# Regrouping the result operands of a two-layer adapter kernel: rank rows of both layers per half, expert rows apart, layer-0 rows gathered by GpSimd

## What is computed

```python
def layer(x, A, B, ids, W, b, eA, eB, rW):           # cut
    c = einsum('bnr,bor->bno', einsum('bni,bri->bnr', x, B[ids]), A[ids])   # rank 16
    alpha = softmax(einsum('bth,eh->bte', c, rW) + const)                   # 4 experts
    z = einsum('bth,erh->bter', c, eA)                                      # rank 8
    return x + c @ W.T + b + 2 * einsum('bter,eor,bte->bto', z, eB, alpha)
x = layer(x, layer 0: 8 adapters, ids 3..7)
x = layer(x, layer 1: 64 adapters, ids 4..50)
```

## Time and profile before

| | |
|---|---|
| time, 3 runs | 365.12 us median, 362.91 to 365.51 |
| profiled execution | span 359.3 us from the first to the last instruction |
| PE busy | 313.8 us, 87% of the span, mean granted clock 0.962 |
| DVE, ACT, POOL busy | 68%, 42%, 25% |
| DMA | 56.15 MB, mean 156 GB/s |

### The profile page before, as it was taken

How to read it: one execution, slowest core, us unless ns; L and a number is a source line. 1 busy time by engine, 2 the same in 40 slices (tenths; PEclk the granted TensorE clock), 3 DMA queues, 4 the chain that set the end, 5 groups by cost and what they waited for, 6 DMA issues and landing times.

```text
span 359.3 us, 6465 instructions
## 1 busy us (share of the span) xinstructions
PE 313.8 (87%) x2056; PEld 296.2 (82%) x2056; DVE 242.6 (68%) x496; ACT 149.4 (42%) x317; POOL 89.6 (25%) x61
## 2 busy tenths in 40 slices
PE   0936568889997999799979999999989998999975
PEld 0935568789997999699979998999989998999854
DVE  5914975788566864787397848784768566864564
ACT  5856833762065404650166206620573065402310
POOL 0014520193015500460026202530244015500000
PEclk9978858969999999999999999999999999999999
DMA  7899426712781078305950387029801880041005
GB/s 284 311 281 332 149 88 200 230 41 68 238 301 40 14 238 288 108 1 156 288 200 0 116 278 249 0 75 298 260 11 51 270 285 36 0 175 61 0 0 234
DMA packets 31524, 56.15 MB, mean 156 GB/s; under 512 B 3793, under 2 KB 21074, under 8 KB 31506
## 3 DMA queue, kind: packets, MB, share of 16 engines
q1 hardware_dynamic: 31506, 55.94, 46.7%
HBM read 39.15 MB, written 16.78 MB: 156 GB/s over the span
## 4 chain that ended last, share of the span: by engine, by line
issue 45%; PE 16%; POOL 14%; DVE 9%; SPq 6%; ACT 4%; DMA 4%; POOLq 0%; ACTq 0%; DVEq 0%
POOL xs_lo L909 12%; PE ps_d L318 4%; PE ps_d L320 3%; PE ps_d L319 3%; POOL a1s_lo L909 2%; DMA abraw<-ab_tab 2%; SPq L222 1%; DMA xraw<-x_in 1%; DVE w1s_lo L676 1%; SPq L233 1%; DVE xs_lo L676 1%; PE ps_h L325 1%; DVE bst_lo L676 1%; SPq L235 1%; ACT m1x_hi L512 1%
## 5 line engine op out<-in xcount | busy, mean ns | idle before, releaser
L909 POOL TENSOR_TENSOR xs_lo<-xraw,xs_hi 128x512 fp32r<-128x512 f32 x48 | 67.7, 1424 | 205.9 <-ACT xs_hi L512 205.9
L318 PE MATMUL ps_d<-w1s_hi,a1s_hi 128*128 128x384 f32 (+1 forms) x216 | 73.4, 340 | 9.5 <-DVE w1s_lo L676 9.5
L320 PE MATMUL ps_d<-w1s_hi,a1s_lo 128*128 128x384 f32 (+1 forms) x216 | 71.3, 330 | 0.0
L319 PE MATMUL ps_d<-w1s_lo,a1s_hi 128*128 128x384 f32 (+1 forms) x216 | 71.0, 329 | 0.0
L895 DVE SCALAR_TENSOR_TENSOR xraw<-ps_d,bsum,xraw 128x512 f32<-128x512 f32 x62 | 46.2, 750 | 26.1 <-PE ps_d L320 26.1
L318 PEld LDWEIGHTS ps_d<-w1s_hi,a1s_hi 128*128 128x128 f32 x216 | 42.3, 196 | 10.1 <-issue 8.4
L318 PE MATMUL ps_p<-xs_hi,bst_hi 128*128 128x256 f32 x128 | 39.4, 307 | 7.4 <-DVE xs_lo L676 3.6
L512 ACT ACTIVATE xs_hi<-xraw 128x512 fp32r<-128x512 f32 x64 | 37.3, 622 | 14.1 <-PE ps_p L320 8.5
L319 PEld LDWEIGHTS ps_d<-w1s_lo,a1s_hi 128*128 128x128 f32 x216 | 42.0, 195 | 0.0
L320 PEld LDWEIGHTS ps_d<-w1s_hi,a1s_lo 128*128 128x128 f32 x216 | 41.8, 194 | 0.0
L319 PE MATMUL ps_p<-xs_lo,bst_hi 128*128 128x256 f32 x128 | 37.9, 296 | 0.0
(11 more groups left out here) (154 smaller groups left out, 661.5 us busy)
## 6 DMA issues: line engine op xcount, KB each, us to landing
xraw<-x_in SPq DMA_DIRECT2D x32, 512.0 KB, 5.9
out<-xraw SPq DMA_DIRECT2D x32, 512.0 KB, 3.8
xraw<-w SPq DMA_DIRECT2D x16, 512.0 KB, 6.1
abraw<-ab_tab SPq DMA_DIRECT2D x64, 128.0 KB, 2.5
b0raw<-b_tab SPq DMA_DIRECT2D x64, 64.0 KB, 2.3
b0raw<-a SPq DMA_DIRECT2D x1, 512.0 KB, 3.6
lp<-exp SPq DMA_DIRECT2D x4, 69.0 KB, 7.3
cm<-exp_in SPq DMA_DIRECT2D x1, 144.0 KB, 6.6
```

Source lines behind the costliest of these rows:

```text
L318: pe.matmul(acc, lh, rh, start=first, stop=False, skip_group_check=True)
L319: pe.matmul(acc, lh, rl, start=False, stop=False, skip_group_check=True)
L320: return pe.matmul(acc, ll, rh, start=False, stop=final, skip_group_check=True)
L909: return pool.tensor_tensor(dst, whole, high.bitcast(F32), ALU.subtract)
```

## The change

- The row operands are regrouped. `res` holds, for each half, 128 rank rows: 64 of layer 1 (made in the step, as before) and 64 of layer 0, of the adapters that the 4 sequences of the half use. Their coefficients are `cf` (c1 in the rows of layer 1, c0 in those of layer 0), two buffers that alternate by step. The scattered `k1` is still made, for `route(0)` and `q`.
- The expert rows stand apart: `ew_hi` has the 64 expert rows twice, `ew_lo` their low parts and 64 zero rows; `ce` holds the high parts of the 64 coefficients and below them the low parts. So the expert part of a tile is two 512-column matmuls, and that of `q` too (`hle`).
- A result tile is thus 2 x 3 matmuls of 256 columns and 2 of 512 (before: 3 of 512 and 6 of 256); `q` is 3 + 2 of 512 (before 3 of 512 and 6 of 256).
- The layer-0 rows go once to a table in DRAM (`m0_tab`, 1 MB), and GpSimd gathers them: in each step, once PE has ended the results of the step before (`d_done`), it loads 8 adapter numbers to registers and issues 8 DMAs of 16 rows x 8 KB (128 KB), ahead of its low parts of x.
- The `start_results` tiles now need c1, so in the last step all five stand behind `route(1)`. ACT and DVE write an expert coefficient in one instruction of 512 columns in place of two of 256, DVE has one low part less behind `hts`. `zs` and `lp` share the new buffer `misc`, whose clearing moves into the prologue.

```diff
-E0ROWS = (slice(HR_, HR_ + LR), slice(0, LR))
-E1ROWS = (slice(HR_ + LR, P), slice(LR, 2 * LR))
+EHIGH = (slice(0, LR), slice(LR, 2 * LR))
+ELOW = (slice(2 * LR, 3 * LR), slice(3 * LR, P))
...
-        m0s = split("m0s", [P, D])
+        ew_hi, ew_lo = split("ew", [P, D])
         hr = sb("hr", [P, KT, 2, HC], F32R)
-        m1x = split("m1x", [P, 2, D])
+        res = sb("res", [P, 2, 2, D], F32R)
...
-        c0s = split("c0s", [P, TOK])
+        cf = [sb(f"cf{i}", [P, 2, TOK], F32R) for i in range(2)]
+        ce = sb("ce", [P, TOK], F32R)
...
-        hts = tuple(t[:, 0:P] for t in c0s)
-        hls = split("hls", [P, 2, P])
+        hle = sb("hle", [P, 2, P], F32R)
...
+        m0_tab = nc.dram_tensor("m0_tab", (ADAPT0, RANK, 2, D), F32)
+        m0s = (res[:, 0, 0, :], res[:, 0, 1, :])
...
+                if k == 3:
+                    sp.wait_ge(m0_lo, len(WIDE_PARTS))
+                    sp.dma_start(m0_tab[:].rearrange("a r h n -> (a r) h n"), res[:, 0, :, :].bitcast(F32)
+                                 ).then_inc(m0_kept, 16)
...
-                    for e, n in enumerate(experts):
-                        r0 = E0ROWS[0].start + e * ER
-                        sp.dma_start(rows_raw[r0:r0 + ER, :],
-                                     exp0_rows[bass.ds(n, 1)].rearrange("a r o -> (a r) o")
-                                     ).then_inc(rows_in, 16)
-                    sp.dma_start(rows_raw[E1ROWS[0], :], exp1_rows).then_inc(rows_in, 16)
+                    for rows0, rows1 in (EHIGH, ELOW):
+                        for e, n in enumerate(experts):
+                            r0 = rows0.start + e * ER
+                            sp.dma_start(rows_raw[r0:r0 + ER, :],
+                                         exp0_rows[bass.ds(n, 1)].rearrange("a r o -> (a r) o")
+                                         ).then_inc(rows_in, 16)
+                        sp.dma_start(rows_raw[rows1, :], exp1_rows).then_inc(rows_in, 16)
...
-            sp.wait_ge(rows_lo, 2)
+            sp.wait_ge(rows_lo, 1)
...
-                product(ps_s[:], part(hts, ALL, ALL), part(k1, ALL, ALL), True, False)
-
-                pe.wait_ge(l_lo, 4 * g + 2)
-                for half in range(2):
-                    cols = slice(half * HALF, (half + 1) * HALF)
-                    mm = product(ps_s[:, cols], part(hls, ALL, half, ALL), part(k2, ALL, cols), False, True)
-                mm.then_inc(q_done, 1)
+                product(ps_s[:], hts, part(k1, ALL, ALL), True, False)
+
+                pe.wait_ge(l_lo, 2 * g + 1)
+                pe.matmul(ps_s[:], hle[:, 0, :], ce[:], start=False, stop=False, skip_group_check=True)
+                pe.matmul(ps_s[:], hle[:, 1, :], ce[:], start=False, stop=True, skip_group_check=True
+                          ).then_inc(q_done, 1)
                 banks = result_banks(last)
 
-                def from_layer0(m):
-                    product(banks[m % len(banks)][:], part(m0s, ALL, slice(m * P, (m + 1) * P)), part(k1, ALL, ALL),
-                            True, False)
+                def from_layers(m):
+
+                    pe.wait_ge(m1_lo, 6 * g + (2 if m < 3 else 6))
+                    for half in range(2):
+                        cols = slice(half * HALF, (half + 1) * HALF)
+                        product(banks[m % len(banks)][:, cols],
+                                (res[:, half, 0, m * P:(m + 1) * P], res[:, half, 1, m * P:(m + 1) * P]),
+                                part(coefs, ALL, cols), half == 0, False)
 
                 def start_results(tiles):
 
                     for m in tiles:
                         if m < 3:
                             pe.wait_ge(m1_lo, 6 * g + (4, 4, 6)[m])
-                        from_layer0(m)
+                        from_layers(m)
 
                 if last:
-                    start_results((0, 1, 3))
+                    pe.wait_ge(m0_picked, 16 * GROUP * (g + 1))
                 else:
                     project(g + 1, 0)
                 pe.wait_ge(f1_lo, 2 * g + 2)
-                route(1, k2, f1s)
+                route(1, coefs, f1s)
+                pe.wait_ge(m0_picked, 16 * GROUP * (g + 1))
                 if last:
-                    start_results((4, 2))
+                    start_results((0, 1, 3, 4, 2))
                 else:
                     project(g + 1, 1)
                 pe.wait_ge(l_done, 2 * g + 2)
                 turn()
                 if not last:
                     start_results(range(3))
-                pe.wait_ge(l_lo, 4 * g + 4)
+                pe.wait_ge(l_lo, 2 * g + 2)
+                if isinstance(g, int) and g == 0:
+                    pe.wait_ge(rows_lo, 1)
                 for m in range(KT):
                     if m >= len(banks):
                         pe.wait_ge(d_out, KT * g + (m + 1 - len(banks)))
-                        from_layer0(m)
-                    for half in range(2):
-                        cols = slice(half * HALF, (half + 1) * HALF)
-                        mm = product(banks[m % len(banks)][:, cols], part(m1x, ALL, half, slice(m * P, (m + 1) * P)),
-                                     part(k2, ALL, cols), False, True)
+                        from_layers(m)
+                    for w in (ew_hi, ew_lo):
+                        mm = pe.matmul(banks[m % len(banks)][:], w[:, m * P:(m + 1) * P], ce[:], start=False,
+                                       stop=w is ew_lo, skip_group_check=True)
                     mm.then_inc(d_done, 1)
...
-                act.wait_ge(rows_in, 16 * (EXP + 1))
-                for half in range(2):
-                    copy(m1x[0][L0ROWS[half], half, :], rows_raw[L0ROWS[0], :]).then_inc(rows_hi, 1)
+                act.wait_ge(rows_in, 16 * 2 * (EXP + 1))
+                copy(ew_hi[:], rows_raw).then_inc(rows_hi, 1)
...
-                    for half in range(2):
-                        rows, cols = (E0ROWS, E1ROWS)[layer][half], slice(half * HALF, (half + 1) * HALF)
-                        copy(k2[0][rows, cols], ps_t[rows, cols]).then_inc(l_hi, 1)
+                    copy(ce[EHIGH[layer], :], ps_t[EHIGH[layer], :]).then_inc(l_hi, 1)
...
+                if first:
+                    act.wait_ge(m0_kept, 16)
...
+            dve.memset(ew_lo[HR_:P, :].bitcast(F32), 0.0)
...
-                dve.memset(lp[:], 0.0).then_inc(init_done, 1)
-                dve.wait_ge(init_done, 2)
...
-                dve.wait_ge(rows_hi, 2)
-                for half in range(2):
-                    low(m1x[1][L0ROWS[half], half, :], rows_raw[L0ROWS[0], :], m1x[0][L0ROWS[0], 0, :]
-                        ).then_inc(rows_lo, 1)
+                dve.wait_ge(rows_hi, 1)
+                low(ew_lo[0:HR_, :], rows_raw[0:HR_, :], ew_hi[0:HR_, :]).then_inc(rows_lo, 1)
...
-                    for half in range(2):
-                        rows, cols = (E0ROWS, E1ROWS)[layer][half], slice(half * HALF, (half + 1) * HALF)
-                        dve.wait_ge(l_hi, 4 * g + 2 * layer + half + 1)
-                        low(k2[1][rows, cols], ps_t[rows, cols], k2[0][rows, cols]).then_inc(l_lo, 1)
+                    dve.wait_ge(l_hi, 2 * g + layer + 1)
+                    low(ce[ELOW[layer], :], ps_t[EHIGH[layer], :], ce[EHIGH[layer], :]).then_inc(l_lo, 1)
...
-                low(hts[1][:], ps_t[:, 0:P], hts[0][:])
-                for half in range(2):
-                    rows = E0ROWS[half]
-                    ins = low(hls[1][rows, half, :], ps_t[rows, P:2 * P], hls[0][rows, half, :])
-                ins.then_inc(ht_lo, 1)
+                low(cf[1 - par][:, 1, HT], ps_t[:, 0:P], cf[1 - par][:, 0, HT])
+                low(hle[EHIGH[0], 1, :], ps_t[EHIGH[0], P:2 * P], hle[EHIGH[0], 0, :]).then_inc(ht_lo, 1)
...
+            def pick_m0(g):
+
+                layer0 = nc.values_load_multi_w_load_instructions(
+                    ids[0:1, bass.ds(g * GROUP, GROUP)], (mybir.EngineType.Pool,), min_val=0,
+                    max_val=ADAPT0 - 1)[1]
+                for b, n0 in enumerate(layer0):
+                    half = b // HSEQ
+                    r0 = L0ROWS[half].start + (b % HSEQ) * RANK
+                    pool.dma_start(res[r0:r0 + RANK, half, :, :],
+                                   m0_tab[bass.ds(n0, 1)].rearrange("a r h n -> (a r) h n")).then_inc(m0_picked, 16)
+
             split_x(0, 0, 0, range(CH))
             split_x(0, 0, 1, (0, 2))
             split_a(0)
+            pool.wait_ge(ids_in, 16)
+            pool.wait_ge(m0_kept, 16)
+            pick_m0(0)
             pool.wait_ge(w1_hi, POOL_CHUNK + 1)
             low(w1s[1][:, POOL_CHUNK, 0:D], w1raw[POOL_CHUNK], w1s[0][:, POOL_CHUNK, 0:D]).then_inc(w1_lo_pool, 1)
 
             def body(g, par, last):
+                if not (isinstance(g, int) and g == 0):
+                    pool.wait_ge(d_done, KT * g)
+                    pick_m0(g)
```

81 lines of the change are left out of this document (43 added, 38 removed).

## The result

The changed kernel took 386.69 us (median of 4, 384.67 to 389.12) against 364.27 (4, 362.91 to 365.51): ratio 1.0643, interval 1.0577 to 1.0709. The forecast of 373.0 had the direction right; the time lies outside its range (357 to 383). The profiled execution has a span of 387.4 us against 359.3. These two spans lie further apart (28.1 us) than the medians (22.4): nearly every execution on record takes 1.6 to 2.1 us more than its span, so the profiled one before was a short one, some 361 us, and the one after was the longest of its four (389.12).

A forecast was written before the change was run, and what follows sets the result against it. A ring from POOL's a1s_lo through SP's gather to PE's `turn()` was taken to bound the kernel. Six turns +12.4 us, the rest -4.6: span 359.3 + 7.8 = 367.1, plus 5.8 gives 373 us, range 357 to 383.

The forecast's parts named there:

- Step 6: Step 0 and prologue: less ACT and DVE work saves 2.0 us; table store and first POOL gather cost nothing.
- Step 4: Landing of SP's gather: POOL's 1 MB of layer-0 transfers delays it by 0.9 us a step, bounds 0 and 3.5.
- What bounds the kernel now: PE is 87% busy but waits at `turn()` in every one of steps 1 to 6; the ring sets the step.
- the ring: Cycle of 37.08 us a step: POOL's a1s_lo, SP's gather, its landing, ACT and DVE, PE's `turn()`, next a1s_lo.
- Steps 1 and 2: PE's result tiles 1.86 us shorter a step, beside the ring; q -0.25 and one low part -0.29 on it.
- Step 3: POOL's layer-0 gather: 8 DMA issues at 1 us each, from 0.58 to 2.42, hidden by POOL before its first xs_lo.
- POOL becomes the ring: Rival: POOL's issues cost 2 us or more, low parts of x come late; about 383 us, chance 0.14.
- Step 5: PE's gap at `turn()` grows to 3.3 to 4.8 us; the clock falls to 1.2 GHz behind it: +1.7 a step.
- Step 7 and the results of step 6: End of the kernel: last step -0.7 us, including +0.9 for the clock; results of the kernel's step 6 -1.9.
- The sum: Whole span: six turns of the ring +12.4 us, prologue and end -4.6, together +7.8, giving 367.1.
- clock holds: Rival: behind `turn()` the longer gap doesn't lower the clock; 362 us, 356 if transfers cost nothing; chance 0.30.
- Columns count: Rival: there is no ring, PE's columns set the time, every step saves 2.1 to 2.4 us; 347 us, chance 0.06.

The follow-up runs named there:

- a_late: Changed kernel with the first layer-0 gather on GpSimd issued after its W1 chunk and after W1's last chunk has landed: 381.09 us.
- a_nopick: Changed kernel without the layer-0 gathers of steps 1 to 7 (all steps use step 0's rows): 369.13 us, ratio 1.0227 to the kernel before.
- a_tiny: Changed kernel with the same waits and issues, but each layer-0 DMA of steps 1 to 7 moves 4 KB instead of 128: 367.44 us, ratio 1.0141.
- a_mid: Changed kernel with each step's 8 layer-0 DMAs moved behind POOL's third low part of x: 408.72 us, ratio 1.1264 to the kernel before.
- a_spread: Changed kernel; in steps 1 to 7 the 8 layer-0 DMAs write 128 partitions of 1 KB instead of 16 of 8 KB: 370.03 us, ratio 1.0104.
- a_whole: Changed kernel; in steps 1 to 7 one DMA moves the whole 1 MB table into 128 partitions in place of 8 DMAs: 372.30 us, ratio 1.0254.

## Why the prediction went wrong, step by step

Two steps failed. Step 6 priced the first gather in the prologue at nothing; its term is off by 10.5 of the 20.3 us by which the spans miss, and some 4.7 of these come back in a_late, where that gather goes out later. Step 4 followed the picks to SP's gather and not to the stores and x loads, and priced them by their bytes. The sizes of the clock terms (steps 5 and 7) were too small besides.

- **What bounds the kernel now**: right. Cutting the ring took 9.0 of PE's 10.2 us at `turn()`, all of ACT's 13.8 us for abraw and 3% of the time away.
- **Steps 1 and 2** (fewer matmuls): right in size. -2.11 us of PE's work for each step were forecast, -2.02 a turn appear once nothing hides them. On the ring -0.54 was forecast; -0.4 is measured (a_nopick against before: -0.20 ahead of `turn()`, -0.23 behind it where the clock is full).
- **Step 3** (POOL's issues): 1 us each was taken, 0.55 was measured (4.41 for 8), SP's price, which the step had named as its lower bound. Nothing follows: a_tiny shows that they are hidden. The 1.5 us that this price was to add through the landing didn't come either. "POOL becomes the ring" was false here; in a_mid, with the picks at another place, PE does wait for POOL.
- **Step 4** (what the transfers do to SP's gather): this step failed, in its path and its size. +0.9 us through the landing of the gather was forecast. The landing is 0.2 us later than without picks: they begin when the gather has been issued. The step asked only for the one transfer on the ring that I had seen there. Next in the queues are the stores of `out`, on which the x loads wait, for which ACT waits ahead of the softmax. And 1 MB was priced at the 298 GB/s of a gather into 128 partitions, though the picks go into 16. Ahead of `turn()` they cost 1.6 us a turn; spread over 128 partitions nothing that could be seen.
- **Step 5** (gap and clock): right in mechanism, somewhat small in size. The waits at `turn()` grew to 28.3 us in 6, the clock fell to 1.2 GHz behind each. That costs 12.72 - 10.60 = 2.1 us a turn against 1.7. Of the 3.3 us by which a turn grew it is the largest part: -0.4 for the savings, +1.6 for the transfers, +2.1 for the clock. Without picks the clock falls in only three turns of six and costs 0.9.
- **Step 6** (prologue): failed. -2.0 forecast, +8.5 measured. "The first gather on POOL lies before its W1 chunk, which PE needs late" asked only for POOL's time, not for what its transfers do to the others. They hold the engines at 113 to 124 GB/s, W1's last chunk can be used 8.9 us after its issue instead of 3.4, and PE waits. a_late puts this down to the picks and not to the expert rows or the store of the table. With the first pick late or wide 3 to 8 us come back; what else is in the 8.5 isn't settled.
- **Step 7 and the results of step 6**: -2.6 forecast, -0.2 measured. The saving is there when the clock holds: a_nopick and a_spread need 46.5 and 46.4 us from the last a1s_lo to the end, 49.6 before. PE waits the same 2.3 us before `route(1)` in both, in the changed kernel (2.32 at 367.78), in a_tiny and in a_whole; but in these last three the clock falls behind it (0.66 over 367 to 377, where a_nopick has 1.00 in the like stretch), and they need 49.3 to 49.4. So the fall costs 2.9 us here, where 0.9 was taken, and it isn't tied to the picks: a_tiny moves nearly no data, a_spread moves it all. Why it falls in one and not in the other stays open.
- **The sum**: spans 367.1 forecast, 387.4 measured, 20.3 off: 10.5 in the prologue, 7.4 in the six turns, 2.4 at the end. The medians are only 13.7 off, and that is luck: the 5.8 us by which the median stood above the span before were some 2 of time outside the span and 3.8 because a short execution had been profiled, and the longest of four was profiled after.
- **Rivals**: "clock holds" fell, since the clock fell behind all six gaps. "Columns count" fell too: a_nopick has the fewer columns and no picks, and its turn of 38.26 us is no shorter than before. It is what happens when the ring is cut.
